# Value products with two stationaries per head in a fused attention and feed-forward kernel

## The reference

```python
qkv = shift_tokens(x) @ Wqkv[i]                  # 128 -> 3 x 1024, 16 heads of 64
q, k = l2norm(q) * q_scale[i], l2norm(k) * k_scale[i]
q = q * cos * scale + rotate_half(q) * sin * scale
k = k * cos / scale + rotate_half(k) * sin / scale
sim = einsum('bhwie,bhwje->bhwij', bq, bk2) * 8   # windows of 32, the own and the one before
attn = softmax(where(mask, -max, sim), -1)
out = einsum('bhwij,bhwje->bhwie', attn, bv2)
x = out @ Wo[i] + x
xn = layernorm(shift_tokens(x)) * ln_g[i] + ln_b[i]
a, gate = split(xn @ W1[i] + b1[i], 2, -1)
x = a * gelu(gate) @ W2[i] + b2[i] + x
```

## Time and profile before

| | us |
|---|---|
| median of 3 runs | 3135.85 |
| lowest, highest | 3133.73, 3137.84 |
| the profiled execution: its own time | 3140.72 |
| its span | 3138.9 |
| TensorE busy in the span | 3047.6 (97%) |
| VectorE | 3011.6 (96%) |
| ScalarE | 2692.7 (86%) |
| GpSimd | 2554.7 (81%) |

### The profile page before, as it was taken

The page is one execution under the profiler, slowest core; times in us unless marked ns, Lnnn a source line. Parts: engine busy times, 40 slices in busy tenths (PEclk is TensorE's granted clock), DMA queues, the critical chain, the costliest instruction groups (busy, mean ns, idle before and its releaser), DMA issues.

```text
span 3138.9 us, 168648 instructions
## 1 busy us (share of the span) xinstructions
PE 3047.6 (97%) x71268; PEld 2184.2 (70%) x71268; DVE 3011.6 (96%) x5981; ACT 2692.7 (86%) x5251; POOL 2554.7 (81%) x2803
## 2 busy tenths in 40 slices
PE   6997999999999999999999999999999999999996
PEld 3553777777777777777777777777777777777775
DVE  6997999999999999999999999999999999999995
ACT  5995888888888888888888888888888888888885
POOL 6986888888888888888888888888888888888883
PEclk8998999999999999999999999999999999999998
DMA  3001222223222223222223222223222223222221
GB/s 83 10 10 30 57 52 59 56 52 89 62 52 62 53 52 91 60 54 61 53 56 88 59 58 57 52 60 86 57 62 53 52 62 89 52 62 53 55 60 52
DMA packets 151240, 182.27 MB, mean 58 GB/s; under 512 B 51668, under 2 KB 74258, under 8 KB 151186
## 3 DMA queue, kind: packets, MB, share of 16 engines
q1 hardware_dynamic: 151186, 181.55, 22.3%
HBM read 21.32 MB, written 2.10 MB: 7 GB/s over the span
## 4 chain that ended last, share of the span: by engine, by line
PE 91%; POOL 3%; issue 2%; ACT 2%; DVE 1%; SPq 1%; DMA 0%; POOLq 0%; ACTq 0%; DVEq 0%
PE bank L1518 11%; PE bank L1475 9%; PE bank L1444 8%; PE bank L1546 7%; PE bank L1453 6%; PE bank L1563 5%; PE bank L1408 5%; PE bank L1528 5%; PE bank L1487 5%; PE bank L1554 5%; PE bank L1495 5%; PE bank L1508 5%; PE bank L1501 4%; PE bank L1422 4%; PE bank L1436 2%
## 5 line engine op out<-in xcount | busy, mean ns | idle before, releaser
L1167 DVE TENSOR_REDUCE sm<-sq 128x32 f32<-128x2048 f32 x192 | 437.0, 2276 | 0.0
L1518 PEld LDWEIGHTS bank<-wo,oT 128*128 128x128 f32 x3072 | 372.9, 192 | 91.7 <-issue 90.1
L1518 PE MATMUL bank<-wo,oT 128*128 128x128 f32 x3072 | 374.2, 275 | 0.8 <-ACT gl L839 0.8
L580 POOL TENSOR_TENSOR qk<-qk,rn 128x512 f32<-128x512 f32 x192 | 200.1, 1042 | 213.2 <-DVE rn L1124 213.2
L1475 PEld LDWEIGHTS bank<-PT,vs 64*64 64x64 f32 x18432 | 288.9, 135 | 94.5 <-issue 93.8
L625 POOL TENSOR_TENSOR P<-P,rowsum 128x512 f32<-128x512 f32 x192 | 200.1, 1042 | 154.4 <-DVE rowsum L1202 154.3
L1475 PE MATMUL bank<-PT,vs 64*64 64x32 f32 (+1 forms) x18432 | 311.0, 220 | 4.2 <-issue 4.2
L1546 PEld LDWEIGHTS bank<-cst,qk 32*128 32x128 f32 x12288 | 206.7, 137 | 147.5 <-issue 147.2
L1444 PEld LDWEIGHTS bank<-qkT 64*32 64x32 f32 x24576 | 279.1, 105 | 15.9 <-issue 5.7
L1444 PE MATMUL bank<-qkT 64*32 64x64 f32 x24576 | 282.6, 225 | 4.6 <-issue 4.6
L637 POOL TENSOR_TENSOR qk<-ta,tb 128x512 f32<-128x512 f32 x192 | 245.5, 1279 | 5.8 <-DVE tb L1212 5.8
(11 more groups left out here) (177 smaller groups left out, 9365.5 us busy)
## 6 DMA issues: line engine op xcount, KB each, us to landing
vs<-vt SPq DMA_DIRECT2D x1152, 128.0 KB, 2.4
wqkv<-L_ffn_Wqkv SPq DMA_DIRECT2D x18, 512.0 KB, 3.7
zm<-zm SPq DMA_DIRECT2D x192, 31.8 KB
wo<-L_ffn_Wo SPq DMA_DIRECT2D x6, 512.0 KB, 4.9
z_sb<-x SPq DMA_DIRECT2D x4, 512.0 KB, 6.1
ctxb<-ctx SPq DMA_DIRECT2D x32, 64.0 KB, 1.8
w<-L_ffn_W SPq DMA_DIRECT2D x6, 341.0 KB, 3.2
out<-x_sb SPq DMA_DIRECT2D x7, 256.0 KB, 2.7
```

Of the source, the lines that this page charges most:

```text
L1167: v_.tensor_reduce(sm[:, :], sq[:, :].rearrange("p (h d) -> p h d", d=DH), AX.X, ALU.add).then_inc(s["d_sumsq"], 1)
L1518: ins = t_.matmul(bank[7][:, 384:512], oT[:, c, :], wo[:, 2 * (c % 4) + c // 4, :], start=c == 0, stop=c == PAIRS - 1)
```

## The change

**Value products.** Each head has two stationaries: tokens 0 to 63 and tokens 64 to 127. The first multiplies 96 queries (windows 0 to 2), the second 64 (windows 2 and 3). Window 2 gets its share from both, so the products accumulate in PSUM. For this PT becomes PTA (96 columns) and PTC (64); in the columns of window 2, ScalarE multiplies the rows of either half with 0 or 1 (`C_HALF`), and masks and scores of window 2 have their two key windows in exchanged order. `shift_v` has two stretches in place of three, so four transfers a unit.

**Roots.** The sum of squares is limited from below by a reduction over (sum, constant) pairs. The Newton step is rn*(3 - s*rn^2), with a factor 0.5 in the rotation table: ScalarE squares rn, GpSimd multiplies with s, ScalarE forms 3-x, GpSimd multiplies into rn. VectorE's four operations go.

**Orders and lags.** Value products and output projection lag by 4, the feed-forward part by 5, the k projections by -1. The order of all engines is new, and SyncE's order at the layer seams.

```diff
             def shift_v(u, par):
                 for r in (0, 1):
                     wait(sp, f"a_v{r}", done(u))
                     wait(sp, "p_AV", count(2, u - 2, 2))
                     rows = slice(64 * r, 64 * r + 64)
-                    for j in range(3):
-                        sp.dma_start(vs[rows, par, j, :], vt[32 * j:32 * j + 64, par, r, :]).then_inc(s[f"l_v{par}"], 16)
+                    for j in range(2):
+                        sp.dma_start(vs[rows, par, j, :], vt[64 * j:64 * j + 64, par, r, :]).then_inc(s[f"l_v{par}"], 16)
...
+                u, on, p = unit(n, k, 1)
+                if on:
+                    wait(pool, "a_n2", done(u))
+                    g.tensor_tensor(rn[:, p, :], rn[:, p, :], n2[:, :], ALU.mult).then_inc(s["g_rn"], 1)
...
+                    g.tensor_tensor(n1[:, :], sc[:, :], n0[:, :], ALU.mult).then_inc(s["g_n1"], 1)
...
                 u, on, p = unit(n, k, 0)
                 if on:
-                    wait(act, f"l_v{p}", 96 * ((u - 2) // 2) + 96 if isinstance(u, int) else (u >> 1) * 96)
+                    wait(act, f"l_v{p}", 64 * ((u - 2) // 2) + 64 if isinstance(u, int) else (u >> 1) * 64)
                     wait(act, "p_v0", done(u))
                     a_.activation(vt[:, p, 0, :], bank[0][:, :], ACT.Copy).then_inc(s["a_v0"], 1)
...
+                    a_.activation(n2[:, :], n1[:, :], ACT.Identity, scale=-1.0, bias=three[:, 0:1]).then_inc(s["a_n2"], 1)
...
-                    a_.activation(PT[:, :, 0:64], bank[4][:, :].rearrange("p (h q) -> p h q", h=PAIRS), ACT.Copy).then_inc(s["a_PT0"], 1)
...
-                    a_.activation(PT[:, :, 64:128], bank[5][:, :].rearrange("p (h q) -> p h q", h=PAIRS), ACT.Copy).then_inc(s["a_PT1"], 1)
...
+                    a_.activation(PTA[:, :, 0:64], bank[4][:, :].rearrange("p (h q) -> p h q", h=PAIRS), ACT.Copy).then_inc(s["a_PA0"], 1)
...
+                    a_.activation(PTC[:, :, 32:64], bank[5][:, :].rearrange("p (h q) -> p h q", h=PAIRS)[:, :, 32:64], ACT.Copy).then_inc(s["a_PC1"], 1)
...
+                    a_.activation(PTA[:, :, 64:96], bank[5][:, :].rearrange("p (h q) -> p h q", h=PAIRS)[:, :, 0:32], ACT.Copy, scale=cst[:, C_HALF:C_HALF + 1]).then_inc(s["a_PA1"], 1)
...
+                    a_.activation(PTC[:, :, 0:32], bank[5][:, :].rearrange("p (h q) -> p h q", h=PAIRS)[:, :, 0:32], ACT.Copy, scale=cst[:, C_HALF + 1:C_HALF + 2]).then_inc(s["a_PC0"], 1)
...
+                    a_.activation(n0[:, :], rn[:, p, :], ACT.Square).then_inc(s["a_r2"], 1)
...
-                    v_.scalar_tensor_tensor(n1[:, :], n0[:, :], 1.0, rn[:, p, :], ALU.mult, ALU.mult).then_inc(s["d_nr2"], 1)
...
-                    v_.scalar_tensor_tensor(rn[:, p, :], n1[:, :], 1.5, rn[:, p, :], ALU.add, ALU.mult).then_inc(s["d_rn"], 1)
...
-                    v_.scalar_tensor_tensor(sm[:, :], sm[:, :], NORM_MIN2, sm[:, :], ALU.max, ALU.max).then_inc(s["d_nr0"], 1)
...
-                    v_.scalar_tensor_tensor(n0[:, :], sm[:, :], -0.5 * LN_UP, rn[:, p, :], ALU.mult, ALU.mult).then_inc(s["d_nr1"], 1)
...
+                    v_.tensor_reduce(sc[:, :], sm[:, :, :], AX.X, ALU.max).then_inc(s["d_nr0"], 1)
...
+                u, on, p = unit(n, k, 4)
+                if on:
+                    wait(pe, "a_tr1", done(u + 2))
...
+                    for i in range(4):
+                        for r in range(2):
+                            for e in range(2):
+                                kr = slice(64 * r, 64 * r + 64)
+                                hc = 128 * i + 64 * e
+                                ins = t_.matmul(bank[4 + r][64 * e:64 * e + 64, 128 * i + 0:128 * i + 96],
+                                                vs[kr, p, 0, hc:hc + 64], PTA[kr, 4 * e + i, :],
+                                                start=i == 0, stop=False, skip_group_check=True)
+                    ins.then_inc(s["p_AV0"], 1)
...
+                                ins = t_.matmul(bank[4 + r][64 * e:64 * e + 64, 128 * i + 64:128 * i + 128],
+                                                vs[kr, p, 1, hc:hc + 64], PTC[kr, 4 * e + i, :],
+                                                start=False, stop=True, skip_group_check=True)
```

More of the change, by code:

```diff
@@ L458, in _ @@
                     load_o(layer + 1)
+                if not last:
                     shift_v(end + 2, 0)
-                    load_b2(layer + 1)
             store(6, 9)
@@ L629, in slot @@
                     edge(pool, u, "d_rec", done(u))
[L630 to L642, removed]
+                    pr = P[:, p, 512:1024].rearrange("p (h t) -> p h t", t=DH)
+                    g.tensor_tensor(pr, pr, rowsum[:, 8:16].unsqueeze(2).to_broadcast([128, 8, DH]), ALU.mult).then_inc(s["g_P1"], 1)
                 u, on, p = unit(n, k, -3)
@@ L888, in slot @@
                     a_.activation(rn[:, p, :], lns[:, :], ACT.Exp, scale=-0.5).then_inc(s["a_rn"], 1)
+                u, on, p = unit(n, k, -1)
+                if on:
+                    wait(act, "p_qk2", done(u))
+                    edge(act, u, "d_sumsq", done(u - 1))
+                    a_.activation(sq[:, 1024:1536], bank[0][:, :], ACT.Square, scale=LN_UP ** 0.5).then_inc(s["a_sq2"], 1)
                 u, on, p = unit(n, k, 1)
@@ L1528, in slot @@
                     t_.matmul(bank[0][:, :], zsT[:, p, :], wqkv[:, 0:512], start=True, stop=True).then_inc(s["p_qk0"], 1)
+                u, on, p = unit(n, k, 5)
+                if on:
+                    wait(pe, "a_zn", done(u))
+                    edge(pe, u, "a_zs", done(u + 6))
+                    wait(pe, "l_w1", 16 * layer_of(u) + 16)
+                    for j, (o, m_) in enumerate(FCH):
+                        ins = t_.matmul(bank[7][0:m_, 128 * j:128 * j + 128], w1[:, FF + o:FF + o + m_], znT[:, :], start=True, stop=True)
+                    ins.then_inc(s["p_gate"], 1)
@@ new lines, in slot @@
+                u, on, p = unit(n, k, -1)
+                if on:
+                    wait(pe, "a_v1", done(u - 1))
+                    edge(pe, u, "a_zs", done(u))
+                    if isinstance(u, int) and u == 0:
+                        pe.wait_ge(s["x_add"], 4 * B)
+                    t_.matmul(bank[1][:, :], zsT[:, p, :], wqkv[:, 512:1024], start=True, stop=True).then_inc(s["p_qk1"], 1)
+                u, on, p = unit(n, k, 5)
+                if on:
+                    edge(pe, u, "a_zn", done(u))
+                    for j, (o, m_) in enumerate(FCH):
+                        ins = t_.matmul(bank[6][0:m_, 128 * j:128 * j + 128], w1[:, o:o + m_], znT[:, :], start=True, stop=True)
+                    ins.then_inc(s["p_a"], 1)
@@ new lines, in slot @@
+                u, on, p = unit(n, k, 4)
+                if on:
+                    wait(pe, "a_gelu", done(u - 1))
+                    edge(pe, u, "a_AV0", done(u))
+                    edge(pe, u, "a_AV1", done(u))
+                    edge(pe, u, "a_zs", done(u + 5))
+                    wait(pe, "l_wo", 16 * layer_of(u) + 16)
+                    for c in range(PAIRS):
+                        ins = t_.matmul(bank[7][:, 384:512], oT[:, c, :], wo[:, 2 * (c % 4) + c // 4, :], start=c == 0, stop=c == PAIRS - 1)
+                    ins.then_inc(s["p_y"], 1)
@@ L1547, in slot @@
                     ins.then_inc(s["p_tr"], 1)
-                u, on, p = unit(n, k, 4)
+                u, on, p = unit(n, k, -1)
+                if on:
+                    edge(pe, u, "a_zs", done(u))
+                    edge(pe, u, "d_rot0", done(u))
+                    wait(pe, "l_wk", 16 * layer_of(u) + 16)
+                    t_.matmul(bank[0][:, :], zsT[:, p, :], wqkv[:, 1024:1536], start=True, stop=True).then_inc(s["p_qk2"], 1)
+                u, on, p = unit(n, k, 5)
                 if on:
```

547 lines of the change are left out of this document (277 added, 270 removed), and 10 rows, old and new, of the table names.

## The result

The changed kernel takes **3254.42 us** (median of 4 runs, 3248.22 to 3259.44), the kernel before 3135.91 us in the same comparison: 1.0373 times as long, 95% interval 1.0358 to 1.0387. That is slower, as forecast, and 41 us more than the 3213 of the prediction. It lies within the range of 3150 to 3270, but 9 us above the band of 3180 to 3245 that had most of the chance.

The account below looks back on a forecast made before the run. TensorE was taken to bound the kernel at 14.66 us a slot; products -0.28 and wait +0.67 give +0.39, over 188 slots +73 us. With +4 for seams, 3,140.7 becomes 3,218, less 5 is 3,213 us; range 3,150 to 3,270.

Parts of the forecast that it names:

- restart: TensorE resuming from an empty array after standing for bank 0: 0.20 us a slot, as a return from small tiles costs.
- TensorE sets the pace: Kernel before: the chain through one slot is TensorE pieces only, 14.66 us; VectorE has 0.2 us to spare.
- The products, -0.28: Value products on TensorE: 64 loads instead of 96 take 1.25 us instead of 1.53, saving 0.28 us a slot.
- The wait.: ScalarE's copy to vt waits for same-slot shift transfers; TensorE stands 0.47 us plus 0.20 restart: +0.67 us a slot.
- A: Time in the slot at which the value products end; the prediction counts the transfers, copy and first q/k projection from it.
- The slot.: TensorE's work of 14.38 us plus 0.67 for the wait: 15.05 us, +0.39 a slot, in 188 slots +73 us.
- Seams, +4: Five layer seams: a 512 KB load issued just ahead of a shift costs up to 1 us each, +4 us.
- VectorE, -1.7 us, worth nothing: Four small operations go, one reduction comes: VectorE falls about 1.7 us a slot to near 12.8; not bounding, no gain.
- ScalarE 14.0 and GpSimd 13.0: Work in us a slot after the added operations, both below TensorE's 14.4; ScalarE with the smallest margin.
- Rival 1: The wait before the vt copy doesn't bind; TensorE runs at 14.38 us a slot: 3,087 us; chance 0.14.
- Rival 2: The wait binds, and the value products gain nothing (slot 15.33 us) or ScalarE becomes the bound: 3,266 us; chance 0.16.
- Rival 3: TensorE's stall only eats the products' gain, 0.28 us instead of 0.67: 3,136 us, no change; chance 0.06.

## Why the prediction was right, point by point

The mechanism was right: the wait, its place in the slot and its parts were found where the prediction had put them. The size was too small: 3254 is nearer to the 3266 of the second rival than to the forecast's 3213. The range reached so far because that rival had the products gain nothing (1.53 us). A part of that came true (1.33, where 1.25 was expected); the rest of the miss is the restart, the first slots and the tail, which the upper end did not name. That they fitted in as well is in part luck. Of the signs named beforehand, the gap (0.47), ScalarE's wait (1.36) and the issues came as forecast; the period (15.19, not 15.0 to 15.1), the products' piece (1.33, not 1.2 to 1.3) and VectorE (13.9, not 12.8) did not.

- **TensorE sets the pace** held: 500.00 of 500 in the earlier trace rows, no time for VectorE's relief alone (the roots in the kernel before), and the slot of the versions with two slots in the loop is TensorE's work plus its gaps (with six transfers, the fallen clock too).
- **The products, -0.28**: measured 0.82+0.51=1.33 against 1.53, so -0.20 (-0.25 with the wait gone: 0.82+0.46). The load-limited half was right, 0.51 us for 32 records. The 96-column half was worked out by columns, 0.65, and takes 0.82, 26 ns a record instead of 20; the tenth added for filling the array covers half of that. The dearer piece of 1.75 that columns alone would give did not come. (The 96 and 64 that the prediction calls products are records, two for each of the 48 and 32 products in the code; the sums are the same.)
- **The wait.** Last landing A+4.30, measured 4.18 (the fourth issue starts at A+1.83 instead of 1.90, and lands 2.34 us after that instead of 2.4). Bank free A+4.95, measured 4.96. TensorE there at A+4.48, measured 4.49. ScalarE standing 1.4 us, measured 1.36. The idle 0.47 was right. The restart was put at 0.20, by the returns from small tiles; after standing idle the piece takes 1.12, and 0.86 without the gap (1005.03 in the run with the split semaphore), so 0.26. **+0.67 became +0.73.**
- **The slot.** 14.66-0.20+0.73=15.19, against 15.05. Two terms of the sum were mis-sized, both the same way, by 0.08 us (the products) and 0.06 us (the restart), times some 190 slots. Over the 177 slots the difference to before is 102.4 us, against 69+4 by the prediction: this is 29 of the 38 us by which the span was missed. Another 5 are the first 14 slots, counted at the loop's 0.39 though they vary (one takes 18.33), and 5.5 the tail, within the 10 that were allowed; the start gives 2.6 back. The remaining 4 of the 41 us are the 5 that were taken off to get from the profiled execution to the median: here the two are 0.9 apart.
- **Seams, +4**: the longer slots hold 4.5. That SyncE's weight loads ahead of a shift are the reason was not tried, so the match may be chance.
- **VectorE, -1.7 us, worth nothing**: it falls from 494 to 458 in 500 us with slots that are longer, about 13.9 us a slot, not 12.8. With the roots alone in the old order it fell by 1.3 us a slot, not 1.7. Here the zn operation (L1286) grew from 343 to 1293 ns and took back 0.95. In the slot shown it stands beside a GpSimd operation and ends just behind it (1011.89 and 1011.74):

```profile
1010.56 1.33 DVE L1286 SCALAR_TENSOR_TENSOR zn<-zm,mv,rstd 128x128 f32<-128x128 f32 x1
1010.47 1.27 POOL L667 TENSOR_TENSOR qk<-ta,tb 128x512 f32<-128x512 f32 x1
```

The rows agree with the Trainium skill's rule (SBUF - State Buffer, section SBUF: two separate sides) that VectorE with two SBUF inputs is locked out for a whole GpSimd instruction: by it, the lockout moved with the order instead of going away. It isn't shown apart from other causes, and TensorE did not wait for it. (From rows 4, the part of the 1.7 us that would be waiting is 0.79+0.58=1.4, not 1.5.)

- **ScalarE 14.0 and GpSimd 13.0**, off the path. Measured 439 and 419 in 500 us, 13.3 and 12.7 a slot. Right that they don't bound.
- **Rival 1, the wait doesn't bind**: false. SyncE's issues take 0.5 to 0.6 us each here too. Its price was nearly right: without the wait the change gives 3106, where I had 3087.
- **Rival 2**: ScalarE is not the bound (the split semaphore), and the products gained 0.20. **Rival 3**: the stall is 0.73, not 0.28.

What stays open: the price of fetching code was not measured by itself, and the reason of the longer seam slots was not looked for.

## What to carry to other kernels

A lag is a buffer's age. Before a consumer is put one slot later, write down for every buffer it reads which unit's refill waits for it, and who waits for that refill: with two buffers, a lag of one more turned 12 us of slack into a loop of issue, landing and copy within one slot. A counter that is too coarse can make the wait: here one semaphore for each half gave back 148 us, without a byte of memory. And when work is added to an engine that doesn't bound, look at what stands behind it there: 0.42 us of lateness in front of the pacing engine cost more than the products gained, until something that was ready was put ahead.

## What the runs showed of the hardware that was not expected

- A loop body of four slots instead of two: 576 code packets instead of 38, and 415 us more for the same work, a part of it with the clock fallen (0.96).
- With TensorE gaps of 1.8 us in a slot of 16.5, the clock fell in 45 of 177 slots, at 1.7 us each; with gaps of 0.47 it stayed at 1.00 from 420 to 3000 us.
- Transfers issued one after the other land well apart, though they share the queue: with the split semaphore the first two of four had landed 2.86 us after the first issue began, at the latest; in the changed kernel the last landed after 4.16.
- The same VectorE operation (zn, 128x128) took 343 ns in the kernel before, 537 with the roots alone in the old order, and 1293 in the new order.
